# The last phase's down products in a macaron FFN–scan–FFN kernel: weights stationary for six of the seven

## What is computed

```python
x = x + 0.5 * ffn(layernorm(x), w_gate, w_up, w_down)
x = x + attn(layernorm(x), W, lam_logit, eta, gamma, beta)   # z = xW, four decayed scans of z, layernorm
x = x + 0.5 * ffn(layernorm(x), w_gate, w_up, w_down)

def ffn(x, w_gate, w_up, w_down):
    gated = silu(x @ w_gate.T) * (x @ w_up.T)
    return gated @ w_down.T
```

## Time and profile before

| | us |
|---|---|
| median of 3 runs | 1016.31 (1016.15 to 1016.5) |
| the profiled execution's own time | 1016.25 |
| its span, first to last instruction | 1014.5 |
| PE busy in it | 1009.2 (99%) |
| DVE / ACT / POOL busy | 723.2 / 425.8 / 188.8 |
| ending: start of batch 0, end of batch 19 | 953.39, 1010.99 |

### The profile page before, as it was taken

The page is one execution under the profiler, slowest core; times in us unless marked ns, Lnnn a source line. Parts: engine busy times, 40 slices in busy tenths (PEclk is TensorE's granted clock), DMA queues, the critical chain, the costliest instruction groups (busy, mean ns, idle before and its releaser), DMA issues.

```text
span 1014.5 us, 13275 instructions
## 1 busy us (share of the span) xinstructions
PE 1009.2 (99%) x4796; PEld 850.8 (84%) x4796; DVE 723.2 (71%) x1067; ACT 425.8 (42%) x681; POOL 188.8 (19%) x219
## 2 busy tenths in 40 slices
PE   9999999999999999999999999999999999999998
PEld 8888888888888888888888888888888888888998
DVE  7755765598988687857978877786686456654673
ACT  6645445456433622223833354232283443333350
POOL 4123343115300200210421020002040222200000
PEclk9999999999999999999999999999999999999999
DMA  6588877769766545646856764554578799864255
GB/s 207 220 319 320 311 254 263 261 209 278 255 228 233 187 159 170 220 142 222 261 188 212 242 209 145 187 175 146 181 263 260 250 332 331 312 228 166 86 185 187
DMA packets 75792, 228.41 MB, mean 225 GB/s; under 512 B 6608, under 2 KB 25040, under 8 KB 68048
## 3 DMA queue, kind: packets, MB, share of 16 engines
q1 hardware_dynamic: 75152, 226.52, 65.8%
q10 hardware_dynamic: 576, 1.05, 0.3%
HBM read 173.02 MB, written 54.53 MB: 224 GB/s over the span
## 4 chain that ended last, share of the span: by engine, by line
PE 99%; DMA 0%; DVE 0%; POOL 0%; ACT 0%; issue 0%; SPq 0%; DVEq 0%; ACTq 0%
PE ps_a L1814 8%; PE ps_a L1816 8%; PE ps_a L1815 8%; PE ps_b L1814 7%; PE ps_b L1816 7%; PE ps_b L1815 7%; PE ps_d L1814 7%; PE ps_d L1816 7%; PE ps_d L1815 7%; PE ps_c L1816 6%; PE ps_c L1814 6%; PE ps_c L1815 6%; PE aux L1816 3%; PE aux L1814 3%; PE aux L1815 3%; PE ps_d L2021 1%
## 5 line engine op out<-in xcount | busy, mean ns | idle before, releaser
L1214 DVE TENSOR_TENSOR tmp<-tmp,ps_c 128x512 f32<-128x512 f32 x59 | 40.4, 685 | 120.6 <-PE ps_c L1816 120.5
L1814 PE MATMUL ps_a<-xt,gu 128*128 128x512 f32 x304 | 118.3, 389 | 0.0
L1815 PE MATMUL ps_a<-xt,gu 128*128 128x512 f32 x304 | 118.3, 389 | 0.0
L1816 PE MATMUL ps_a<-xt,gu 128*128 128x512 f32 x304 | 118.3, 389 | 0.0
L1815 PE MATMUL ps_b<-xt,gu 128*128 128x512 f32 x286 | 111.3, 389 | 0.0
L1814 PE MATMUL ps_b<-xt,gu 128*128 128x512 f32 x286 | 111.3, 389 | 0.0
L1816 PE MATMUL ps_b<-xt,gu 128*128 128x512 f32 x286 | 111.3, 389 | 0.0
L1814 PE MATMUL ps_d<-dn,hid 128*128 128x512 f32 (+1 forms) x256 | 92.8, 363 | 0.0
L1816 PE MATMUL ps_d<-dn,hid 128*128 128x512 f32 (+1 forms) x256 | 92.8, 362 | 0.0
L1815 PE MATMUL ps_d<-dn,hid 128*128 128x512 f32 (+1 forms) x256 | 92.8, 362 | 0.0
L1815 PE MATMUL ps_c<-xt,gu 128*128 128x512 f32 x236 | 91.8, 389 | 0.0
(11 more groups left out here) (275 smaller groups left out, 2321.4 us busy)
## 6 DMA issues: line engine op xcount, KB each, us to landing
dn<-dn_kept SPq DMA_DIRECT2D x92, 512.0 KB, 4.1
gu<-gu_kept SPq DMA_DIRECT2D x46, 1024.0 KB, 5.0
gu<-gu_kept SPq DMA_DIRECT2D x46, 768.0 KB, 5.6
gu_kept<-gu SPq DMA_DIRECT2D x14, 1024.0 KB, 4.5
gu_kept<-gu SPq DMA_DIRECT2D x14, 768.0 KB, 4.2
dn_kept<-dn SPq DMA_DIRECT2D x16, 512.0 KB, 5.1
t_kept<-zx SPq DMA_DIRECT2D x16, 512.0 KB, 4.6
dn<-t_kept SPq DMA_DIRECT2D x16, 512.0 KB, 3.7
```

The costliest lines, as they stand in the source:

```text
L1214: dve.tensor_tensor(dst, u3s(si), p5_bank(si)[:, :], ALU.add).then_inc(c22_done, 1)
L1814: pe.matmul(dst, a_hi, b_hi, start=start, stop=False, skip_group_check=chained)
L1815: pe.matmul(dst, a_hi, b_lo, start=False, stop=False, skip_group_check=chained)
L1816: return pe.matmul(dst, a_lo, b_hi, start=False, stop=stop, skip_group_check=chained)
```

## The change

In Q1, Q2, Q5, Q6, Q7 and Q3 the operands change places: 128 columns of the down weights are stationary, and all 512 tokens of a row move. A group of four 256-wide token blocks becomes two 512-wide banks, half as many matmuls with twice the width. Their results lie with features on the partitions, and they have to be turned. Only Q4 stays as it was, in four banks of its own (`q4_ps`), token by token.

What carries the sums out: ACT copies `x_ps` and `z_ps` to SBUF rows (`copy_feature`; of these two copies after Q1, after Q6, after Q5 and after Q7). PE waits for the copies before it adds on the banks. DVE adds what else belongs to a result (`add_feature`, `add_third_link`), turns the sum in 32x32 blocks within its quadrants of 32 partitions (`turn_feature`), and ACT and POOL share 16 copies that carry each block's rows to the quadrant they belong to (`place_feature` on ACT; the first 8, 10 and 8 of 16 for the three results, called jobs). Then DVE adds the result to `x_tok` (`add_result`), and SP stores it.

```diff
+    PLACED_BY_ACT = (8, 10, 8)
...
+        with nc.sbuf_tensor("gu_rows", [P, 14, tokens], F32) as gu_rows:
+            pass
...
+        q4_ps = [ps_d[2], ps_d[3], ps_b, ps_c]
...
+        def feature_rows(job):
+            return (zx_rows[:, 0:2, :], gu_rows[:, 0:4, :], zx_rows[:, 6:8, :])[job]
...
+            if n == SEG + PAIRS + 17:
+                sp.wait_ge(result_added, 1)
+                store_half(2, 0)
+        for job in (1, 2):
+            sp.wait_ge(result_added, job + 1)
+            store_half(4 - job, 1)
...
+            def copy_feature(job, row, banks, semaphore, n):
+                act.wait_ge(semaphore, n)
...
+                for b in range(2):
+                    act.copy(feature_rows(job)[:, row + b, :], banks[b][:, :]).then_inc(feature_copied, 1)
+
+            def place_feature(job):
+                act.wait_ge(feature_turned, (2, 6, 8)[job])
...
+                for q in range(PLACED_BY_ACT[job]):
+                    act.copy(to_token(job, q), from_feature(job, q)).then_inc(act_placed, 1)
...
-                    for n in range(1, 20):
+                    stage_hi_of(1)
+                    stage_hi_of(2)
+                    copy_feature(0, 0, x_ps, first_done, 2 * PAIRS - 1)
+                    for n in range(3, 20):
+                        if n == 13:
+                            copy_feature(2, 0, x_ps, batch_done, ENDING.index((Q6, 3)) + 1)
+                        if n == 14:
+                            copy_feature(1, 2, z_ps, batch_done, ENDING.index((Q5, 3)) + 1)
+                        if n == 18:
+                            copy_feature(1, 0, x_ps, batch_done, ENDING.index((Q7, 3)) + 1)
                         stage_hi_of(n)
+                        if n == 10:
+                            place_feature(0)
+                    place_feature(1)
+                    place_feature(2)
...
+            for job in range(3):
+                pool.wait_ge(feature_turned, (2, 6, 8)[job])
+                for q in range(PLACED_BY_ACT[job], 16):
+                    pool.tensor_copy(to_token(job, q), from_feature(job, q)).then_inc(pool_placed, 1)
...
-                    last = three(unit_half(y_ps if odd else x_ps, t), hid0[:, odd, 0, a], hid0[:, odd, 1, a],
-                                 dn[:, n % DN, odd, 0, :], dn[:, n % DN, odd, 1, :], q == 0 and t % 2 == 0,
-                                 q == PAIRS - 1, True)
+                for b in range(2):
+                    a = slice(b * P, (b + 1) * P)
+                    last = three((y_ps if odd else x_ps)[b][:, :], dn[:, n % DN, odd, 0, a], dn[:, n % DN, odd, 1, a],
+                                 hid0[:, odd, 0, :], hid0[:, odd, 1, :], q == 0, q == PAIRS - 1, True)
...
-                    pe.wait_ge(block_added, {Q6: 2, Q3: 8, Q7: 6, Q4: 10}[w])
+                    pe.wait_ge(feature_copied, {Q6: 2, Q7: 4, Q3: 6}[w])
...
+                        last = three(banks[b][:, :], dn[:, n % DN, k, 0, a], dn[:, n % DN, k, 1, a],
+                                     xt[:, op, 0, k, :], xt[:, op, 1, k, :], w == Q5 and i == k == 0,
+                                     i == 3 and k == 1, True)
```

More of the change, by code:

```diff
@@ L267, in t_part, with turned_rows, token_rows, result_rows @@
             return zx[:, part, 2:4, :].rearrange("p r (a n) -> p (r a) n", a=2)
+        def feature_rows(job):
+            return (zx_rows[:, 0:2, :], gu_rows[:, 0:4, :], zx_rows[:, 6:8, :])[job]
+        def turned_rows(job):
+            return (zx_rows[:, 2:4, :], gu_rows[:, 4:8, :], zx_rows[:, 0:2, :])[job]
+        def token_rows(job):
+            rows = (zx_rows[:, 4:6, :], gu_rows[:, 8:12, :], zx_rows[:, 2:4, :])[job]
+            return rows.rearrange("p r t -> p (r t)").rearrange("p (s n) -> p s n", s=ST)
+        def result_rows(job):
+            return (x_tok[:, 8:12, 0:HALF], x_tok[:, 12:16, :], x_tok[:, 8:12, HALF:D])[job]
+        def from_feature(job, q):
+            i, j = q // 4, q % 4
+            return turned_rows(job)[32 * i:32 * i + 32, :, j * P:(j + 1) * P].rearrange("p b (s c) -> p b s c", s=ST)
+        def to_token(job, q):
+            i, j = q // 4, q % 4
+            rows = token_rows(job).rearrange("p s (b i c) -> p b i s c", i=4, c=32)
+            return rows[32 * j:32 * j + 32, :, i, :, :]
         def first_rows(i, odd):
@@ L342, in macaron_kernel @@
         batch_done = sem("batch_done")
[L343 removed]
+        unit_done = sem("unit_done")
         turned_x = sem("turned_x")
@@ L546, in store_unit, with store_half @@
                 sp.dma_start(out_v[b, :, q, :], x_tok[:, b * ST + q, :]).then_inc(out_stored, 16)
+            def store_half(b, half):
+                n = slice(half * HALF, (half + 1) * HALF)
+                sp.dma_start(out_v[b, :, :, n], x_tok[:, b * ST:(b + 1) * ST, n]).then_inc(out_stored, 16)
             def store_tile(b):
@@ L1349, in stage_lo_of, with add_feature @@
                                   xt[:, stage_op(n), 0, :, :].bitcast(F32), ALU.subtract).then_inc(stage_lo, 1)
-            def add_block(banks, b, tile, half, semaphore, n, added=0):
+            def add_feature(job, banks, semaphore, n):
                 dve.wait_ge(semaphore, n)
[L1354 to L1364, removed]
+                dve.wait_ge(feature_copied, {0: 2, 2: 4}[job])
+                for b in range(2):
+                    row = feature_rows(job)[:, b, :]
+                    dve.tensor_tensor(row, row, banks[b][:, :], ALU.add).then_inc(feature_added, 1)
@@ new lines, in add_third_link, with turn_feature @@
+            def add_third_link():
+                dve.wait_ge(feature_copied, 8)
+                rows = feature_rows(1)
+                dve.tensor_tensor(rows[:, 2:4, :], rows[:, 2:4, :], rows[:, 0:2, :], ALU.add).then_inc(feature_added, 1)
+            def turn_feature(job):
+                dve.wait_ge(feature_added, (2, 3, 5)[job])
+                if job == 0:
+                    dve.wait_ge(t_stored, 32 * PAIRS)
+                if job == 2:
+                    dve.wait_ge(result_added, 1)
+                for r in range((2, 4, 2)[job]):
+                    dve.transpose(by_block(turned_rows(job)[:, r, :], True), by_block(feature_rows(job)[:, r, :])
+                                  ).then_inc(feature_turned, 1)
@@ new lines, in add_result, with add_unit @@
+            def add_result(job):
+                dve.wait_ge(act_placed, sum(PLACED_BY_ACT[:job + 1]))
+                dve.wait_ge(pool_placed, sum(16 - n for n in PLACED_BY_ACT[:job + 1]))
+                x = result_rows(job)
+                dve.scalar_tensor_tensor(x, token_rows(job), 0.5, x, ALU.mult, ALU.add).then_inc(result_added, 1)
+            def add_unit(t):
+                dve.wait_ge(unit_done, t + 1)
+                dve.wait_ge(result_added, 2)
+                x = x_tok[:, 12 + t, 0:HALF]
+                dve.scalar_tensor_tensor(x, q4_ps[t][:, 0:HALF], 0.5, x, ALU.mult, ALU.add).then_inc(unit_added, 1)
@@ L1789, in _ @@
             s3_of(PAIRS - 1)
-            for b in range(2):
-                add_block(x_ps, b, 2, 0, first_done, 2 * PAIRS - 1)
             stage_lo_of(3)
@@ L1799, in _ @@
             stage_lo_of(6)
+            stage_lo_of(7)
+            add_feature(0, y_ps, first_done, 2 * PAIRS)
+            stage_lo_of(8)
+            turn_feature(0)
+            stage_lo_of(9)
             s4_of(PAIRS - 1)
-            for b in range(2):
-                add_block(y_ps, b, 2, 0, first_done, 2 * PAIRS, b + 1)
-            for n in range(7, 20):
+            stage_lo_of(10)
+            stage_lo_of(11)
+            add_result(0)
+            for n in range(12, 18):
                 stage_lo_of(n)
-                if n in (8, 10, 13, 17):
-                    add_product({8: Q6, 10: Q5, 13: Q7, 17: Q3}[n])
-            add_product(Q4)
+            add_third_link()
+            turn_feature(1)
+            stage_lo_of(18)
+            stage_lo_of(19)
+            add_feature(2, z_ps, batch_done, ENDING.index((Q3, 3)) + 1)
+            turn_feature(2)
+            add_result(1)
+            add_result(2)
+            for t in range(ST):
+                add_unit(t)
         @block.tensor
@@ L1977, in first_block @@
                     pe.wait_ge(c12_done, upto(SETS * LAST + 1))
-                for t in range(ST):
-                    a = slice(t * P, (t + 1) * P)
-                    last = three(unit_half(y_ps if odd else x_ps, t), hid0[:, odd, 0, a], hid0[:, odd, 1, a],
-                                 dn[:, n % DN, odd, 0, :], dn[:, n % DN, odd, 1, :], q == 0 and t % 2 == 0,
-                                 q == PAIRS - 1, True)
+                for b in range(2):
+                    a = slice(b * P, (b + 1) * P)
+                    last = three((y_ps if odd else x_ps)[b][:, :], dn[:, n % DN, odd, 0, a], dn[:, n % DN, odd, 1, a],
+                                 hid0[:, odd, 0, :], hid0[:, odd, 1, :], q == 0, q == PAIRS - 1, True)
                 last.then_inc(first_done, 1)
@@ L1993, in batch @@
```

(26 more changed lines are left out.)

24 lines of the change are left out of this document (13 added, 11 removed).

## The result

| | us |
|---|---|
| before, median of 20 runs | 1016.17 (1015.73 to 1016.56) |
| changed, median of 20 runs | 1017.96 (1017.09 to 1018.66) |
| ratio | 1.0019, 95% interval 1.0012 to 1.0025 |
| predicted | 1015.8, range 1012.9 to 1018.6 |
| changed, profiled execution: own time, span | 1018.10, 1016.3 |

The change costs 1.8 us. That is just inside the 0.2% that the prediction called no change, but clear of the noise, and on the other side of the forecast.

What follows compares the result with a forecast made beforehand. The prediction took PE's own pace as the bound. With most of the 4.0 us gain lost to a new wait, PE's end moved -0.26 us and the last add -0.27: -0.53 in all, 1015.8 us, range 1012.9 to 1018.6.

Steps and rivals of the forecast that it cites:

- What bounds it, and the gain on PE: Whole kernel: PE's pace bounds it, and wider matmuls save 4.0 us if PE never waits.
- PE never waits: Rival for the ending: PE waits not at all or under 2 us, the gain is kept, 1012.0 us; chance 0.18.
- the sum's 1.45: Gain before batch 0: 0.10 us in each of 14 sets, 1.40, and 0.05 in the last pair of blocks.
- The new wait: Before batch 8 (Q7): PE waits 3.75 us for ACT's copies of x_ps, queued behind eight copies between quadrants and two casts.
- The bound below it: Before batch 8: PE waits 2.8 us even if ACT's eight copies cost nothing, since batch 11's cast needs the last s4_of.
- the gain before batch 8 is swallowed: At batch 8: ACT's queue sets the start, so PE's earlier 1.45 us and 8 x 0.16 are given up.
- PE waits 3.75 us: Before batch 8: due at 973.70, begun at 977.45, followed by batches at full pace.
- The wait brings the clock down: Rival behind the pause before batch 8: PE at 1.2 GHz, 2.7 us more a batch, 1018.5 or 1021.2 us; chance 0.16.
- about one batch at the lower level: Behind the pause: how long the slower clock must last to decide the result; less stays within the measurement.
- The other waits: Ending: copies after Q1 and Q5, remainders of batches 3 to 7 and the first result's store come in time, delaying nothing.
- The tail: After Q3: the third result and its store cost nothing; PE's end decides, and the half-wide last add saves 0.27 us.
- even the upper bound: Tail: the third result's add ends at 1009.2 with POOL's copies at 0.762 us, against 1006.8 in the likely case.

Runs made afterwards that it cites:

- e1: The changed kernel with the two copies of x_ps after Q6 moved on ACT ahead of the eight copies between quadrants: 1011.64 us.
- e10: e1 with Q1 and Q2 made with 256-wide matmuls again, as before the change: 1013.40 us.
- e3: The changed kernel with ACT making 4 instead of 8 of the first job's 16 copies between quadrants: 1016.65 us.
- e2: The changed kernel with 13 small float32 matmuls that nobody needs on PE in the pause before batch 8: 1015.58 us.
- e7: The changed kernel with the two copies of x_ps after Q6 right behind ACT's eight copies between quadrants, ahead of batch 11's cast: 1015.57 us.
- e5: The kernel before with the late adds of e4, and 15 small float32 matmuls on PE in the pause: 1020.63 us.
- e6: The changed kernel with the two copies of x_ps after Q6 behind batch 11's cast on ACT, one cast earlier: 1016.56 us.
- e4: The kernel before with the adds that follow Q6, Q5 and Q7 moved later on DVE, so that PE pauses 4.5 us before Q7: 1022.49 us.

## Why the prediction was wrong, point by point

- *What bounds it, and the gain on PE.* Right. Sets of 10.88 us (predicted 10.88), batches of 2.72, and e1 at 1011.64 where "PE never waits" was put at 1012.0. Q1's and Q2's part is 1.43 us in the traces of e1 and e10, for the sum's 1.45.
- *The new wait.* Right in place, releaser and, nearly, in size. The prediction's 3.75 us run from when batch 8 was due to when it began; by the same measure it is 3.88 (due at 973.25, begun at 977.13), and the gap that the profile shows is 3.73. It stands behind eight copies of 0.426 each (predicted 0.425) and two casts. The bound below it was real too: in e3 the cast of batch 11 waited for the last `s4_of`, as was said. That the gain before batch 8 is swallowed, because ACT's queue sets its start, is what e2 measures: with the clock kept, 1015.58, 0.6 us under before, where the sum said 0.5.
- *The step that failed* is how the wait was turned into time: "PE waits 3.75 us" entered the sum at 3.75 us, with the clock at 1.00 behind it. That it would fall was written as a rival, "The wait brings the clock down", at one chance in six and a price of 2.7 us a batch. It fell in all 20 executions (mean clock 0.997 or 0.998); in the profiled one the whole of batch 8 was slow, and that cost 2.64 us. 1015.8 with that is 1018.4. The median is 1017.96 because the executions form two groups of ten: 1017.1 to 1017.8 us at a mean clock of 0.998, and 1018.1 to 1018.7 at 0.997. The profiled one is of the second. The reason given for the low chance, "it is one pause, and matmuls before and after are dense", was no evidence: no row had a pause of PE among dense matmuls, and e7 shows that half the pause is enough most of the time. The kernel before did hold a hint that was not read. It opens with small matmuls that nobody uses (`keep_warm(WARM)`), after 1.56 us of idle time, and these 36 take 7.18 us, 0.20 each, where 26 of the same kind took 3.06 us, 0.12 each, in e2. It proves nothing by itself, since the clock row reads 1.00 there. The rule of the Trainium skill that stood there ("TensorE: Matmul & The Clock Gate", Part 1, half the clock after an idle stretch) agrees with these rows in direction, and should have been given far more than one chance in six. The point from which the prediction let it decide ("about one batch at the lower level") was right, and reached.
- *The other waits.* Right: PE has no other wait in the ending.
- *The tail.* The size of POOL's copies was wrong, 0.731 us on average (0.87 in the first group of eight, 0.69 in the tail) for the 0.45 taken, near the upper bound of 0.762. The third result ended at 1011.3, 2.1 us behind even the upper bound, because Q3 ended 2.3 us later than predicted. It changed nothing: the last add was 0.42 us long, as taken, and the span ends 2.6 us behind it, as before.

What stays open: why the clock comes back sooner in some executions of the same kernel (1017.1 to 1017.8 and 1018.1 to 1018.7 us for the change), and why a pause of 1.8 us is harmless in 3 of 11 and one of 3 us in 2 of 11. Pauses between 1.0 and 1.8 us were not tried. Why POOL's copies are slower in one place than in the other was not tried.

## What to carry to other kernels

When PE runs at 99% and a change gives it a wait, count the wait twice: its length, and the matmuls behind it at half the clock. Here a wait of 0.98 us was free of the second part; from 1.83 us on it mostly came, and cost another 1 to 3 us. Before a queue of small copies is put on an engine, look for the one instruction behind them that releases PE and put it first; here that alone turned 1.8 us lost into 4.6 us won. If the wait can't go, matmuls that nobody needs can hold the clock through it, as in e2 and e5.

## What the runs showed of the hardware that I had not expected

- A pause of PE of 1.83 us between dense matmuls brought the granted clock from 1.00 to 0.50 in 8 of 11 executions, one of 0.98 us in none of 6. In the profiled executions of e6, e7, e3 and e4 the clock fell only after PE had begun again, by 0.2, 0.4, 0.6 and 0.8 us; in the change's it fell during the pause.
- 26 small matmuls of 128 columns, 3.06 us in all, followed by 0.74 us of idle time, kept it at 1.00 in all 11 executions (e2).
- POOL's copies of 32x256 between quadrants took 0.731 us on average, hardly less than the 32x512 ones before the change (0.762). The changed kernel's own 32x512 copies, of the same kind, took 0.911, so the row of another kind was a poor measure. ACT's 32x256 took 0.404 and its 32x512 0.619. POOL's first group of eight took 6.95 us, the one in the tail 5.56.
